# Moving output products, denominators and value products in the written order of an attention and feed-forward kernel

## The reference

```python
q, k, v = heads(xn @ Wq), heads(xn @ Wk), heads(xn @ Wv)       # 16 heads of 64
w = softmax(q @ k.T / 64 + causal)
w = w * clip((key_number + span * 1024) / 33, 0, 1)
w = w / (sum(w) + 1e-8)
attention = concat(w @ v) @ Wo
ffn = dequantised(round(xn / scale)) @ (ternary - 1).T + bias
out = x + attention + ffn
```

## Time and profile before

| | |
|---|---|
| three runs, median | 1027.01 us |
| profiled execution, its own time | 1027.36 us |
| its span in the profile | 1025.6 us |
| PE busy | 989.4 us |
| PE weight loads busy | 636.0 us |
| VectorE busy | 781.4 us |
| GpSimd busy | 735.0 us |
| ScalarE busy | 452.7 us |

### The profile page before, as it was taken

The page is one execution under the profiler, slowest core; times in us unless marked ns, Lnnn a source line. Parts: engine busy times, 40 slices in busy tenths (PEclk is TensorE's granted clock), DMA queues, the critical chain, the costliest instruction groups (busy, mean ns, idle before and its releaser), DMA issues.

```text
span 1025.6 us, 19261 instructions
## 1 busy us (share of the span) xinstructions
PE 989.4 (96%) x7169; PEld 636.0 (62%) x7169; DVE 781.4 (76%) x1753; ACT 452.7 (44%) x600; POOL 735.0 (72%) x646
## 2 busy tenths in 40 slices
PE   3699999999999999999999999999999999999996
PEld 2466666666666666666666666666666666666654
DVE  8778888888788888877768777777877777777752
ACT  2144544444544444544444544444454444454441
POOL 8686766777776677776867676768776667767685
PEclk9599999999999999999999999999999999999998
DMA  6000000000000000000000000000000000000000
GB/s 169 2 2 1 3 2 2 3 2 1 2 22 3 3 2 2 2 3 2 3 12 12 2 3 2 2 2 3 1 2 22 2 2 3 1 2 2 3 1 21
DMA packets 12124, 8.44 MB, mean 8 GB/s; under 512 B 1280, under 2 KB 11520, under 8 KB 12032
## 3 DMA queue, kind: packets, MB, share of 16 engines
q1 hardware_dynamic: 11424, 7.08, 2.5%
q10 hardware_dynamic: 608, 0.14, 0.1%
HBM read 4.33 MB, written 2.10 MB: 6 GB/s over the span
## 4 chain that ended last, share of the span: by engine, by line
PE 92%; DVE 3%; POOL 2%; issue 2%; DMA 1%; ACT 1%; POOLq 0%; SPq 0%; DVEq 0%
PE ring L867 28%; PE pv L884 23%; PE ring L840 10%; PE beside L910 7%; PE ring L827 6%; PE beside L893 6%; PE ring L817 3%; PE ring L818 3%; PE ring L819 3%; POOL psumd L432 1%; DVE rowmax L672 1%; PE beside L906 1%; PE beside L847 1%; DMA x_sb<-in_L_attn_query 0%; POOL psumd L428 0%
## 5 line engine op out<-in xcount | busy, mean ns | idle before, releaser
L488 ACT ACTIVATE prob<-ring 128x1024 f32<-128x1024 f32 (+3 forms) x384 | 297.5, 812 | 350.5 <-PE ring L867 342.3
L432 POOL TENSOR_TENSOR psumd<-psumd,prob 128x1024 f32<-128x1024 f32 (+3 forms) x256 | 429.5, 1678 | 29.2 <-POOL psumd L432 1.3
L668 DVE CUSTOM_DVE_ANT_0 ring<-ring,causal 128x128 f32<-128x128 f32 (+3 forms) x512 | 240.4, 517 | 114.4 <-PE ring L840 114.0
L867 PE MATMUL ring<-q,k 64*128 64x512 f32 (+3 forms) x2304 | 284.7, 353 | 3.6 <-DVE rowmax L672 2.0
L884 PE MATMUL pv<-prob,v 128*64 128x512 f32 (+3 forms) x1536 | 267.0, 490 | 0.0
L407 POOL TENSOR_SCALAR_AFFINE_SELECT prob<-prob 128x256 f32<-128x256 f32 x256 | 104.1, 407 | 198.6 <-ACT prob L488 196.0
L867 PEld LDWEIGHTS ring<-q,k 64*128 64x128 f32 x2304 | 189.8, 186 | 48.8 <-ACT prob L488 10.6
L884 PEld LDWEIGHTS pv<-prob,v 128*64 128x64 f32 x1536 | 104.7, 137 | 154.1 <-issue 141.1
L672 DVE TENSOR_REDUCE rowmax<-ring 128x2 f32<-128x1024 f32 x128 | 153.3, 1219 | 17.4 <-PE ring L840 14.1
L428 POOL TENSOR_TENSOR psumd<-prob 128x768 f32<-128x768 f32 x64 | 134.2, 2097 | 42.4 <-ACT prob L488 37.4
L840 PE MATMUL ring<-k,q 64*128 64x512 f32 (+3 forms) x768 | 143.7, 411 | 6.8 <-ACT k L477 2.4
(11 more groups left out here) (97 smaller groups left out, 865.0 us busy)
## 6 DMA issues: line engine op xcount, KB each, us to landing
x_sb<-in_L_attn_query SPq DMA_DIRECT2D x4, 512.0 KB, 7.1
out<-x_sb SPq DMA_DIRECT2D x8, 256.0 KB, 2.3
kext<-lnw SPq DMA_DIRECT2D x64, 8.0 KB
mrow<-maxrow SPq DMA_DIRECT2D x64, 4.0 KB
wv<-in_L_attn_Wv SPq DMA_DIRECT2D x1, 512.0 KB, 3.5
wo<-in_L_attn_Wo SPq DMA_DIRECT2D x1, 512.0 KB, 7.3
xn_sb<-in_L_attn_Wq SPq DMA_DIRECT2D x1, 448.0 KB, 4.4
xn_sb<-in_L_attn_Wk SPq DMA_DIRECT2D x1, 448.0 KB, 5.1
```

Source lines behind the costliest of these rows:

```text
L432: g.tensor_tensor(acc[:, :, lo:HALF], acc[:, :, lo:HALF], pr[:, :, lo:HALF], ALU.add).then_inc(acc_done, 1)
L488: a.activation(prob[n % NPROB][:, :, lo:HALF], ring[:, slot(f"S{t}", i), :, lo:HALF], ACT.Exp, scale=1.0 / DH).then_inc(exp_done, 1)
L668: last = v.tensor_tensor_reduce(out=ring[:, s, h, 0:n], in0=ring[:, s, h, 0:n], in1=causal[:, HALF - n:HALF], scale=1.0, scalar=MASKED, op ...
L867: last = t_.matmul(ring[:, s, h, lo:HALF], k[p][rows, keys], q[p][rows, cols], start=(at == 0), stop=(at == len(parts) - 1))
```

## The change

Only three strings differ. `PLACE`, `IN_RING` and the like are made from them, so the waits follow.

```diff
-PE_PLAN = ("T Q+ K+ X0 X1 W G11- M0+ M1+ S0 S1 S2 M2+ D1- M3+ V+ S3 S4 M4+ S5 S6 M5+ Y1- M6+ M7+ S7 D0 G3 "
-           "M8+ S8 S9 S10 M9+ Y0 M10+ M11+ S11 G7")
-ACT_PLAN = "Z Qhi+ Khi+ X0 X1 E0 E1 E2 ln1- ex1- E3 E4 E5 E6 E7 ln0 ex0 E8 E9 E10 E11"
-DVE_PLAN = ("Tc Z Qlo+ Klo+ R0+ R1+ X0 X1 W R2+ R3+ t1- Vs+ u1- R4+ o1- R5+ Ya1- q R6+ R7+ t0 u0 R8+ o0 R9+ "
-            "R10+ Ya0 R11+ Rc+")
+PE_PLAN = ("Q+ T K+ X0 X1 W Y0- G11- D1- M0+ M1+ S0 M2+ S1 S2 S3 S4 M3+ M4+ Y1- V+ S5 S6 M5+ D0 M6+ S7 M7+ G3 "
+           "M8+ S8 M9+ S9 S10 S11 M10+ M11+ G7")
+ACT_PLAN = "Z Qhi+ Khi+ X0 X1 ln1- ex1- E0 E1 E2 E3 E4 E5 E6 ln0 ex0 E7 E8 E9 E10 E11"
+DVE_PLAN = ("Tc Z Qlo+ X0 X1 W Ya0- Klo+ R0+ R1+ R2+ t1- u1- o1- R3+ Ya1- R4+ Vs+ R5+ R6+ R7+ t0 R8+ u0 R9+ o0 "
+            "R10+ R11+ Rc+ q")
```

## The result

| | before | changed |
|---|---|---|
| median (4 runs each, same chip) | 1026.28 us | 1061.59 us |
| lowest to highest | 1025.49 to 1027.22 | 1061.12 to 1064.39 |
| ratio to before, 95% interval | | 1.0349 [1.0328, 1.0371] |
| profiled execution, its span | 1027.36, 1025.6 us | 1064.39, 1062.6 us |
| plain turn (17 to 19) | 30.00 us | 30.47 us |

The change makes the kernel 3.5% slower, 35 us. The forecast was 1061 us.

A forecast was written before the change was run, and what follows sets the result against it. PE was taken to pace the kernel, busy 989.4 of 1025.6 us, with every chain link its own. Terms 16.6 + 6.6 + 1.8 + 1.6 + 6.2 - 0.7 + 1.1 + 0.5 = +33.7 on 1027.36 gave 1061 us, range 1043 to 1073.

The forecast's parts named there:

- The wait behind the turned rows: Turns 4, 5, 12, 13, 20, 21: PE idles before Y0 until VectorE's low part: 4 x 2.5 + 2 x 3.3 = +16.6 us.
- a normalisation of 2.95 us: Turns 4 and 12: VectorE's layer-norm work ahead of Qlo takes 2.95 us, so PE stands still for 3.3 us.
- The clock: After the six waits behind the turned rows: four falls to half clock, 1.65 us each, +6.6 us.
- Rival 1: Waits of 2.5 us are too short to lower the clock: 6.6 us goes, 1050 us named; chance 0.22.
- Turn 1: W's result is read by VectorE behind Qlo, with Y0 now directly behind it, so PE waits: +1.8 us.
- Layer-norm turns: Turns 3, 7, 9, 10, 11: D1 waits for Ya0 behind VectorE's normalisation and Qlo: +1.6 us.
- Every turn: Each turn: cheaper kind changes and waits about -1.0 us, dearer ones about +1.3; taken as +0.2 x 31 = +6.2 us.
- VectorE's `R1`, which frees the slot of `S1`, ends at about the same point: Every turn: R1's end coincides with the freeing of S2's slot, within the +0.3 us of waiting given to S2.
- Rival 3: Ring slots become free in time, removing nearly all 45 us of weight-load waits: 1015 us; chance 0.05.
- Rival 2: ln1 and ex1, without slack ahead of E0, delay the exponentials: +0.6 us a turn, 1073 us; chance 0.14.
- The quantisation: Turns 8, 16, 24: step hidden at turn's end saves some 0.9 us, later Ya1, R4, S6 cost 0.7: -0.7 us.
- The end: Turn 31: Y0, G11 and D1 stand ahead of S0, which starts the last chain: +1.1 us (+1.3 in the ledger).

The follow-up runs named there:

- The first experiment: The changed kernel with the turned rows X0 and X1 moved behind V on all three engines: 1039.88 us, ratio 1.0123 to the kernel before.
- e0: Not a name in the kept text, and the text given defines no run of this name, so no change or time can be stated.

## Why the prediction was right, and where its steps were not

**The wait behind the turned rows: right.** Place (line 910 for line 565), cause (one tile `beside`, used by neighbours) and size: 2.38 us for a forecast of 2.5. The first experiment takes it away with nothing else touched, the second brings it with `Y0`'s move alone. The two longer ones were off singly, and that the sum came out (16.3 for 16.6) is luck: turn 4 waited 2.38 instead of 3.3 and turn 12 waited 4.35. The step that failed is "a normalisation of 2.95 us": that is what it took in each such turn of the kernel before, but it is not a constant. In the changed kernel (timeline, turns 4 and 12):

```profile
167.33 2.11 DVE L558 TENSOR_SCALAR xn_sb<-x_sb,mv,rstd 128x128 f32<-128x128 f32 x4
...
422.56 4.15 DVE L558 TENSOR_SCALAR xn_sb<-x_sb,mv,rstd 128x128 f32<-128x128 f32 x4
...
424.29 2.34 POOL L397 TENSOR_TENSOR x_sb<-x_sb,bias_b 128x1024 f32<-128x1024 f32 x1
...
428.49 1.77 PE L910 MATMUL beside<-wo,o 128*128 128x128 f32 x8 [4.35 <-DVE x L565]
```

**The clock: right in price (1.6 us a fall), and in count by luck.** The four of six were picked between none and all, without a row for them. Rival 1 (it stays up) fell. Which waits are followed by a fall isn't settled: turns 13 and 21 had waits of the same 2.38 us and no fall, and in the experiments that kept the six waits it was three of six (`Y0` moved alone; both moved) or four of six (both kernels with the step inside the turn of the new order). Each count is from one execution. The three faster runs of the changed kernel are 2.5 to 3.3 us shorter, at a mean granted clock of 0.981 to 0.984 against 0.978, which fits one or two falls fewer but doesn't show it.

**Turn 1**: +1.3 for 1.8, the same mechanism, a little shorter.

**Layer-norm turns: wrong sign**, -1.5 for +1.6. `D1` did not wait for `Ya0`, since the four normalising instructions took 2.1 to 2.2 us together, not 2.95; in turn 3 `Ya0` ended 0.27 us ahead of `D1`. And the 0.3 us that these turns lost in the old order went. The sum itself was also too high: four turns at 0.6 and one at 1.2, less 0.3 to 0.4 in seven turns, is +0.8 to +1.5, not +1.6.

**Every turn: the right idea, mis-sized**, +0.47 for +0.2. A part of that was in the working: its own terms, 1.3 less 1.0, give +0.3, and it took +0.2, which alone is 3 of the 8 us. Start to start, the units that became cheaper give -1.3 us (`M3` -0.20, `M9` -0.20, `Y0`, `S6`, `V`, `G11` -0.10 or so each, and smaller ones) where I had -1.0. The dearer ones give +1.7 where I had +1.3. Of these the waits at `S10` (+0.46 for 0.3 and an exposed load) and at `M11` (+0.21) are as forecast. The first failed step is "VectorE's `R1`, which frees the slot of `S1`, ends at about the same point": its wait does not coincide with `S2`'s but comes ahead of it, at `S1`, and costs 0.31 (`M2`, 0.37 to 0.68); behind it `S2` does not wait any more. So the size was right and the place wrong. The second is what isn't in the list: `M10` +0.18, and `M7`, `S1` and `S5` +0.08 or so each. The third is `S3`, which was to become 0.1 cheaper and takes 0.10 more.

**Rival 3, slots that become free in time, fell the other way**: the three largest waits of PE's weight loads for slots went from 44.9 to 77.6 us. Only 14 of the 33 us more show in the time; I take the rest to stand in the place of kind changes and load times that PE spent anyway; no run separates these. For the rule of the Trainium skill quoted in the prediction, that weight-load busy time is the better metric, the two traces say little: its share went from 62 to 60% and PE's from 96 to 93%, since the busy times stayed (636.0 and 633.2, 989.4 and 989.6 us) while the span grew.

**Rival 2, the inverse delays the exponentials**, fell too: `S0` starts at 622.37 and its exponential at 623.50, 1.13 later, exactly as before.

**The quantisation: right direction, too small**, -3.0 for -0.7. The 0.9 us of waiting went in each of three turns, as said, and the step, counted as 2.7 us, takes 0.74 at its new place; the +0.7 set against it, "the long `Y1` now pushes `Ya1`, `R4` and `S6`", did not come. Turns 8, 16 and 24 take 32.24, which is 30.47 and two feed-forward products.

**The end**: +2.7 for 1.3. In turn 31, which has no `M` tiles any more, `D0` stands earlier and waits 1.78 us for GpSimd's sums; in the kernel before it did not wait. Behind that the clock fell once more, at 1036.4, for 3.4 us. I had counted falls only behind the six waits. (Both kernels end at 0.50: the one before from 1017.1 on, the changed one from 1056.9.) The stretch up to the end of turn 0 gained 0.5 instead of losing 0.5.

So the sum was right because the largest terms were, and in part by luck: errors of +8 (every turn) and -5 (layer-norm, quantisation) met, and the median that 1061 hits is of runs 2.5 us and more shorter than the one whose ledger comes to +37.0, against +33.7 in the forecast.

## What to carry to other kernels

In an order written by hand, every unit has two prices: its own time, and what it covered where it stood. `D1` and `Y0` looked free to move, since they saved a change of kind elsewhere; between tiles that share a ring of slots they had covered 0.4 and 0.6 us a turn. Look for a moved unit's cover in the waits of its old neighbours, and for a single buffer whose two users become adjacent; a new spread has to be tested together with the moves that it depends on (here `D1`'s and `T`'s).

## What the runs showed of the hardware that I had not expected

**VectorE's normalisation takes 0.33 to 2.38 us for the same shape**, by what GpSimd does beside it. The answers for the line 558, shortest, median and longest in ns, of before and of the changed kernel:

```profile
L558 DVE TENSOR_SCALAR xn_sb<-x_sb,mv,rstd x32: 332/439/1316, 10.5 to 411.8; 128x128 f32<-128x128 f32 x32
```

```profile
L558 DVE TENSOR_SCALAR xn_sb<-x_sb,mv,rstd x32: 332/634/2377, 9.5 to 424.3; 128x128 f32<-128x128 f32 x32
```

From turn 3 on, the instructions of 332 to 338 ns start while GpSimd runs nothing. The others start while one of GpSimd's additions runs and end 0.08 to 0.09 us after it: they take 1.19 to 1.32 us in the kernel before, 0.75 to 0.99 us in the changed one, and the one of 2377 ns lies under the bias addition of 2.34 us (line 397, shown above). The first quantisation step, also of one shape each time, shows the same; before and changed kernel:

```profile
L590 DVE TENSOR_SCALAR fq<-xf,sc x4: 1440/2720/2741, 60.0 to 792.7; 128x1024 f32<-128x1024 f32 x4
```

```profile
L590 DVE TENSOR_SCALAR fq<-xf,sc x4: 740/742/742, 71.5 to 836.6; 128x1024 f32<-128x1024 f32 x4
```

In the kernel before, the three of 2.7 us start 0.2 us into a GpSimd addition of 2.4 us and end 0.56 us after it. In the changed kernel all four start 0.06 us before such an addition ends. So I take some 2 of the 2.71 us of the earlier trace rows, behind which a score tile waited, to be a wait for GpSimd. Line 565, also VectorE's, keeps its 0.67 to 0.69 us throughout, but in the turns nothing of GpSimd's runs beside it. The Trainium skill says in "SBUF — State Buffer", Terms, that VectorE and GpSimd share a pair of ports, which is held for the full instruction while the loser blocks fully. These lengths agree: an instruction that starts under one of GpSimd's lasts until that one ends, and is not slowed in proportion. So a duration of such an instruction, read from one place of a trace, holds only as long as GpSimd's work beside it does.

**A single idle stretch of PE of 2.38 us can be followed by 3.4 us at half the clock (0.50)**, and need not: in the changed kernel it was so behind three of five such waits and behind the one of 4.35 us, with `Y0` moved alone behind three of six.
